# Spreading the score steps of exact attention evenly over the slots

## The chip, the cores and the metric

The kernel runs on one core of one Trainium2 chip. The metric is the device time of one execution in microseconds; lower is better. The engines are TensorE (PE in the profile, PEld its weight loads), VectorE (DVE), ScalarE (ACT), GpSimd (POOL) and SyncE (SP), whose queue issues most of the DMAs. Each engine works through its own list of instructions in order and waits on semaphores where it needs another's result.

## The reference, cut to what matters

Four layers work on x of 4 x 512 x 128 with a context of 4 x 154 x 128. The change touches the attentions of the first two layers alone: the cross attention of L0 and the causal self attention and the cross attention of L1, all with 16 heads of 8 features, softmax exact in float32.

```python
# L0: cross attention over the context
q = (target @ wq).reshape(b, tq, 16, 8); k, v likewise from the context
scores = jnp.einsum('bqhd,bkhd->bhqk', q, k) * (1.0 / np.sqrt(8))
attn = jax.nn.softmax(scores, axis=-1)
out = jnp.einsum('bhqk,bkhd->bqhd', attn, v).reshape(b, tq, d) @ wo + bo
# L1: the same twice, first causal over x itself, then over the context,
#     x = _layernorm(x + _attn(...)) after each, then a mixture of 8 experts
```

Behind them come the experts of L1, two quantised attentions and a feed-forward of L2, and a grouped attention with a feed-forward of L3. The change leaves these alone.

## The kernel before, in words

The three exact attentions times four sequences make 12 *units*, `EXACT_UNITS`: 0 to 3 are L0's cross attentions, 4 to 7 the causal self attentions, 8 to 11 L1's cross attentions. A unit has 4 *groups* of 4 heads.

Each head's scores are computed twice. A *score step* (`scores_exact`) computes scores with the queries on the partitions, only so that `top_exact` on DVE (line 1912) can take the maximum along the keys. A cross unit has 4 steps a group, each of 8 matmuls (lines 1075 and, in L0, 1079) with one reduction of 128 x 616; a self unit has 8 a group, whose widths fall with causality from 512 to 128 keys (lines 1083 and 1085), with reductions of 1024 down to 256 elements. The steps share two pairs of PSUM banks: step i waits until the reduction of step i-2 is done. When a group's last step is reduced, `split_tops` (lines 1921 to 1924, four small DVE operations) splits the maxima into bf16 parts; the item `tops` transposes them on PE (line 963) and ACT copies them out (line 1406).

The second computation has the keys on the partitions. It goes by *slots*: `scores_transposed(w)` (lines 1109 to 1113, for the context's tail 1101 and 1103) fills one of two banks with scores less the maxima, and ACT takes the exponential (line 1468). A group has 5 slots in a cross unit and 10 in a self unit, so there are 320 slots, 20 or 40 a unit. `weigh_batch` (lines 1134 and 1136) multiplies finished exponentials with the values.

PE's order in a slot is written out by hand: `scores_transposed(w)`, the score steps of the slot, the slot's items, the weighing. DVE's order is the slot's reductions (with `split_tops` behind a group's last), then the slot's items. The items of `schedule` carry the rest: K, Q and V are projections; N1, r and N2 normalise the output of the unit before (r are four reciprocals, line 1686; N2 is line 973 on PE and 1690 on DVE); W is its output projection and statistics, M and H its layer norm and transposes; R1 to R3 and G (lines 1007 and 1012) are the routing of the experts.

The steps of a group are computed during the group before: `steps_in_slot(w)` puts them into the first `PER - 3` slots of the group before. In a cross unit that is two steps in each of the group's slots 0 and 1 and none in slots 2 to 4; in a self unit one each in slots 0 to 5, two in slot 6, none in 7 to 9. `tops` stands in slot `per - 2` of the group: slot 3 of 5, or slot 8 of 10.

The first group of a unit is computed in the last group of the unit before it, so its first step needs that unit's keys and queries. These take a long way: items K and Q (slots 0 and 1 of a cross unit, 1 and 2 of a self unit), ACT copies, DVE splits each into three bf16 terms (`split`, lines 1624 to 1626), SP writes the terms to DRAM (line 791) and reads them back stacked, 16 DMAs for the keys (line 773) and then 16 for the queries (line 780). `scores_exact` with i == 0 waits for both.

In a cross unit the last group has slots 15 to 19, in a self unit slots 30 to 39. Slots are numbered from the unit's first below, unless "slot w of 320" is said.

Of the kernel before, what the change touches and what calls it, by code (L numbers as in the profile page):

```python
# [17 lines left out]
GROUPS = HEADS // 4  # L18
# [45 lines left out]
EXACT_UNITS, QUANT_UNITS = range(0, 12), range(16, 24)  # L64
# [10 lines left out]
def is_cross(u):  # L75
    return stage(u) in (L0, CROSS, QCROSS)
# [6 lines left out]
def exact_steps(u):  # L83

    if is_cross(u):
        return [(c, n) for c in range(PAIRS) for n in range(2)]

    return [(2 * g + c, n) for g in range(GROUPS) for n in reversed(range(TILES)) for c in range(2)]
# [16 lines left out]
STEP_BASE, BLOCKS, BATCHES, BATCH_BASE, FIRST_SLOT = {}, [], [], {}, {}  # L105
# [11 lines left out]
PER = {u: (5 if is_cross(u) else 10) for u in EXACT_UNITS}  # L117
PER_GROUP = {u: len(exact_steps(u)) // GROUPS for u in EXACT_UNITS}


def next_group(u, g):
    return (u, g + 1) if g + 1 < GROUPS else (u + 1, 0) if u + 1 in EXACT_UNITS else None


def steps_in_slot(w):

    u, g = BLOCKS[w][:2]
    n = (w - FIRST_SLOT[u]) % PER[u]
    to = next_group(u, g)
    if to is None:  # L130
        return []
    v, h = to
    a, b = (min(PER_GROUP[v], PER_GROUP[v] * m // (PER[u] - 3)) for m in (n, n + 1))
    return [(v, h * PER_GROUP[v] + i) for i in range(a, b)]


def weigh_in_slot(w):
# [229 lines left out]
def build(nc, io, out):  # L367
# [3 lines left out]
    with ctx:  # L371
# [384 lines left out]
        with nc.Block() as block:  # L756
# [146 lines left out]
            def _(pe):  # L903
# [242 lines left out]
                for w in range(EXACT_SLOTS):  # L1146
                    scores_transposed(w)
                    for u, i in steps_in_slot(w):
                        scores_exact(u, i)
                    for it in EXACT_ITEMS.get(w, ()):  # L1150
                        item(*it)
                    if weigh_in_slot(w) is not None:
                        weigh_batch(weigh_in_slot(w))
# [428 lines left out]
            def _(dve):  # L1582
# [348 lines left out]
                for w in range(EXACT_SLOTS):  # L1931
                    for u, i in steps_in_slot(w):
                        top_exact(u, i)
                        if (i + 1) % PER_GROUP[u] == 0:
                            split_tops(u, i // PER_GROUP[u])
                    for it in EXACT_ITEMS.get(w, ()):
                        item(*it)
# [377 lines left out]
```

How the kernel before makes its waits and increments, by code:

```python
            @once.gpsimd  # L706
# [7 lines left out]
                nc.gpsimd.memset(ctxT_tail4[:, :, :, :], 0.0)  # L714
                nc.gpsimd.memset(k_half_ctx.rearrange("p a s c k -> p (a s c k)").bitcast(fp32), 0.0)
                nc.gpsimd.memset(k_tail.rearrange("p a g k -> p (a g k)").bitcast(fp32), 0.0)
                nc.gpsimd.memset(top_cols.rearrange("p a t j c -> p (a t j c)").bitcast(fp32), 0.0)
                nc.gpsimd.memset(pad_rows, 0.0)
                nc.gpsimd.memset(zeros[:, :], 0.0)
                nc.gpsimd.memset(ones_bf[:, :], 1.0)
                nc.gpsimd.memset(picked[:, :, :].rearrange("p t e -> p (t e)"), 0.0)
                for i in range(2):
                    nc.gpsimd.memset(blocks_to[i][:, 0:EXPERTS], 0.0)
                pool.wait_ge(v_cols_cleared, 1)
                wide = v_cols.rearrange("p t (a i j) c -> p (t a) i j c", i=2, j=4)
                for i in range(2):
                    nc.gpsimd.memset(wide[:, :, i, :, 16 + HD * i:16 + HD * (i + 1)], 1.0)
# [1 line left out]
            @once.vector  # L729
            def _(dve):
                dve.wait_ge(cleared, 4)
                for j in range(4):
                    nc.vector.memset(ones[32 * j:32 * j + 3, j, :], 1.0)
                    nc.vector.memset(ones_tail[32 * j:32 * j + 3, 32 * j:32 * j + CTX_TAIL], 1.0)
# [30 lines left out]
                    def read_keys():  # L765
                        sp.wait_ge(k_out, 48 * (u + 1))
                        if u >= 2 and u != SELF * B:
                            sp.wait_ge(scoresT_ready, FIRST_SLOT[u - 1])
```

## Time and profile before

| what | us |
|---|---|
| median of three runs | 1651.88 (1650.27 to 1656.32) |
| profiled execution | 1640.09 |
| its span on the core | 1638.3 |
| mean granted TensorE clock | 0.83 |

| engine | busy us | share |
|---|---|---|
| PE | 1174.7 | 72% |
| PEld | 666.8 | 41% |
| DVE | 1100.5 | 67% |
| ACT | 901.9 | 55% |
| POOL | 678.3 | 41% |

The exact attentions take the first 614 us or so. Busy time of PE counts matmuls whose ends are modelled, so a wait between two matmuls shows only where it is longer than the pipeline. A timeline row gives start, duration, engine, line, operation, output and inputs, shapes, how many instructions it merges, and in brackets the idle time of the engine before it with what ended it. "issue" there is a wait that nothing in the profile is seen to end.

### The profile page before, as it was taken

To read this page: it belongs to the slowest core of one execution; us is meant where nothing else is said; L and a number is where in the kernel's file an instruction comes from. 1 tells how busy PE (TensorE), PEld (TensorE's weight loads), DVE (VectorE), ACT (ScalarE), POOL (GpSimd) and SP (SyncE) were. 2 spreads that over 40 slices of the span, in tenths; PEclk is the share of its full clock that TensorE was granted. 3 is DMA by queue.
4 is the path that set the end of the run, shared out by engine and by line. 5 is a ranking of instruction groups with operands and counts; after the bars stand their busy time and mean duration, and the time that the engine had idled before them with its cause. 6 is when DMAs were issued, how large, how long until landed. Compare 5 with 4: busy or idle time off the path is not lost.

```text
span 1638.3 us, 27753 instructions
## 1 busy us (share of the span) xinstructions
PE 1174.7 (72%) x8832; PEld 666.8 (41%) x8832; DVE 1100.5 (67%) x3127; ACT 901.9 (55%) x2546; POOL 678.3 (41%) x1048
## 2 busy tenths in 40 slices
PE   2698989999978788784534354544438778888888
PEld 1354445555534338782111121122215534453545
DVE  2466676676667775367989899977764566666533
ACT  1344545445544446456767778888882254545642
POOL 5201100110111141545888878877771245344420
PEclk9899999999999999896555555555559899999999
DMA  5322332120153211216655557665560112111000
GB/s 165 64 47 57 62 92 65 61 72 17 32 106 91 47 40 38 83 51 161 118 99 108 98 109 124 116 109 105 106 108 14 26 38 54 30 31 43 6 1 26
DMA packets 263825, 115.53 MB, mean 71 GB/s; under 512 B 215928, under 2 KB 252672, under 8 KB 261504
## 3 DMA queue, kind: packets, MB, share of 16 engines
q1 hardware_dynamic: 258720, 107.34, 31.3%
q0 software_dynamic: 2048, 4.20, 0.9%
q10 hardware_dynamic: 2912, 2.22, 0.4%
q8 instruction: 71, 1.16, 0.3%
q14 instruction: 74, 0.61, 0.1%
HBM read 38.54 MB, written 16.45 MB: 34 GB/s over the span
## 4 chain that ended last, share of the span: by engine, by line
PE 36%; DVE 19%; POOL 18%; issue 14%; ACT 9%; DMA 2%; SPq 1%; POOLq 0%; DVEq 0%; ACTq 0%
POOL arena L2221 10%; ACT arena L1521 5%; DVE minus_top L1912 4%; PE acc L1136 3%; PE misc L973 3%; PE trans L1109 2%; POOL inv_total L2210 2%; PE trans L1113 2%; PE misc L979 2%; PE trans L1260 2%; PE score L1272 2%; PE score L1075 2%; PE score L1274 1%; DVE top_score L1994 1%; PE score L1083 1%
## 5 line engine op out<-in xcount | busy, mean ns | idle before, releaser
L2221 POOL TENSOR_SCALAR arena<-arena,inv_total 128x512 f16<-128x512 f32 (+1 forms) x512 | 299.6, 585 | 57.4 <-DVE inv_total L1988 16.2
L1912 DVE TENSOR_REDUCE minus_top<-score 128x4 f32<-128x616 f32 (+4 forms) x256 | 197.3, 805 | 165.8 <-PE score L1079 65.2
L2084 POOL TENSOR_TENSOR rstd<-spread,minus_half 128x4 f32<-128x4 f32 x36 | 37.6, 1045 | 539.2 <-DVE spread L1602 469.9
L1521 ACT ACTIVATE arena<-score,minus_top,exp_scale 128x512 f32<-128x512 f32 (+1 forms) x340 | 210.4, 625 | 17.5 <-POOL arena L2221 7.5
L1468 ACT ACTIVATE arena<-trans 128x512 f32<-128x512 f32 x240 | 141.3, 597 | 136.0 <-PE trans L1113 133.5
L1559 ACT ACTIVATE arena<-arena,minus_top 128x154 f32<-128x154 f32 x256 | 105.1, 412 | 132.4 <-DVE minus_top L2053 132.2
L1217 PE MATMUL score<-arena 32*128 32x512 bf16 (+1 forms) x340 | 69.0, 458 | 143.2 <-ACT arena L1521 142.1
L1994 DVE TENSOR_REDUCE top_score<-score 128x2 f32<-128x1024 f32 (+1 forms) x128 | 135.6, 1060 | 0.6 <-PE score L1217 0.5
L2241 POOL TENSOR_TENSOR arena<-arena,inv_total 128x512 f32<-128x512 f32 x64 | 66.6, 1040 | 146.9 <-DVE inv_total L2061 133.0
L1113 PE MATMUL trans<-arena 128*128 128x512 bf16 (+3 forms) x384 | 123.0, 329 | 0.0
L1521 ACT ACTIVATE arena<-trans,minus_top,exp_scale 128x154 f32<-128x154 f32 (+1 forms) x172 | 105.5, 620 | 16.3 <-POOL arena L2221 11.7
L2048 DVE CUSTOM_DVE_ANT_0 arena<-score,arena 128x154 f32<-128x154 f32 x256 | 66.1, 314 | 62.8 <-PE score L1297 62.5
L1977 DVE TENSOR_SCALAR arena<-arena 128x1024 bf16<-128x1024 f16 x192 | 102.7, 535 | 6.1 <-DMA arena<-arena 6.0
L1075 PE MATMUL score<-arena 128*128 128x154 bf16 x512 | 69.3, 244 | 35.9 <-issue 27.8
L1217 PEld LDWEIGHTS score<-arena 32*128 32x128 bf16 x340 | 14.2, 102 | 194.6 <-ACT arena L1521 177.5
L1512 ACT ACTIVATE minus_top<-top_score,exp_scale 128x2 f32<-128x2 f32 (+1 forms) x192 | 56.5, 294 | 61.0 <-DVE top_score L1994 60.6
L1217 PE MATMUL trans<-arena 32*128 32x154 bf16 (+1 forms) x172 | 34.9, 454 | 71.9 <-ACT arena L1521 71.8
L1468 ACT ACTIVATE arena<-trans,arena 128x512 f32<-128x512 f32 x80 | 53.9, 689 | 56.2 <-PE trans L1113 55.4
L1136 PE MATMUL acc<-arena 128*32 128x512 f32 (+3 forms) x768 | 80.2, 505 | 2.3 <-ACT arena L1468 2.3
L1236 PE MATMUL acc<-arena 128*32 128x128 bf16 x1536 | 59.3, 307 | 28.0 <-DVE oT L2002 15.5
L1109 PE MATMUL trans<-arena,late 128*128 128x512 bf16 (+3 forms) x256 | 76.5, 301 | 0.3 <-ACT arena L1406 0.3
L1486 ACT ACTIVATE arena<-score,arena 128x128 f32<-128x128 f32 x184 | 52.2, 369 | 40.7 <-PE score L1173 40.6
(283 smaller groups left out, 3046.7 us busy)
## 6 DMA issues: line engine op xcount, KB each, us to landing
arena<-q_terms SPq DMA_DIRECT2D x176, 64.0 KB
late<-arena SPq DMA_DIRECT2D x128, 64.0 KB, 2.0
q_terms<-arena SPq DMA_DIRECT2D x36, 128.0 KB
late<-k_terms SPq DMA_DIRECT2D x64, 64.0 KB
arena<-arena SPq DMA_TRANSPOSE x192, 3.0
by_expert<-zeros SPq DMA_DIRECT2D x2, 1472.0 KB, 14.3
arena<-by_expert SPq DMA_DIRECT2D x10, 256.0 KB, 3.0
from_expert<-arena SPq DMA_DIRECT2D x10, 256.0 KB, 2.6
```

What stands on the lines that cost most here:

```text
L1075: ins = nc.tensor.matmul(dst, q_stack[:, u % 2, c, t * P:(t + 1) * P], k_half_ctx[:, u % 2, s, c, 0:CTX], start=True, stop=(stage(u) != L0))
L1109: nc.tensor.matmul(dst, keys, q_stack[:, u % 2, h // 2, q0:TOKENS], start=True, stop=False)
L1113: ins = nc.tensor.matmul(dst, ones[:, j, :], top_rows[:, g % 2, q0:TOKENS], start=False, stop=True)
L1136: ins = nc.tensor.matmul(acc[32 * j:32 * j + 32, q0:TOKENS], v_cols[:, k, 4 * g + j, :], src, start=(b % half == 0 and k == 0), stop=(last ...
L1217: ins = nc.tensor.matmul(quant_score[i % 3][:, j, z * n:(z + 1) * n], qT_codes[r:r + 32, u % 2, t * P:(t + 1) * P], k4_codes[r:r + 32, u % ...
L1468: nc.scalar.activation(expT[w % SLOTS], trans[w % 2][:, :], ACT.Exp, bias=bias)\
L1521: ins = nc.scalar.activation(probs[:, i % 3, j, of], quant_score[i % 3][:, j, of], ACT.Exp, bias=minus_top[:, at_col:at_col + 1], scale=ex ...
L1559: ins = nc.scalar.activation(gq_exp_p[:, i % 3, h, :], shifted[:, i % 3, h, :], ACT.Exp, bias=minus_top[:, at_col:at_col + 1], accum_out=t ...
L1912: nc.vector.tensor_reduce(dst, src, axis=AX.X, op=ALU.max, negate=True).then_inc(top_ready, 1)
L1977: nc.vector.tensor_scalar(pT_codes[:, of, :, :].rearrange("p k q -> p (k q)"), pT_raised[:, of, :, :].rearrange("p k q -> p (k q)"), -HALF ...
L1994: nc.vector.tensor_reduce(of_step(top_score, i), src, axis=AX.X, op=ALU.max, negate=True).then_inc(quant_top, 1)
L2221: ins = nc.gpsimd.tensor_scalar(codes[:, (i - 1) % CODE_SOURCES, j, to], probs[:, (i - 1) % 3, j, of], inv_total[:, at_col:at_col + 1], HA ...
```

## The change

A table, computed once, takes the place of the formula. The score steps of a group go one by one to evenly spaced slots of a stretch that is as long as the group in which they were, but lies `AHEAD` = 3 slots sooner.

```diff
+AHEAD = 3
+
+
+def place_steps():
+
+
+    slots = {}
+    for u in EXACT_UNITS:
+        for g in range(GROUPS):
+            to = next_group(u, g)
+            if to is None:
+                continue
+            v, h = to
+            start = FIRST_SLOT[u] + g * PER[u]
+            first, end = max(0, start - AHEAD), start + PER[u] - AHEAD
+            for i in range(PER_GROUP[v]):
+                slots.setdefault(first + ((end - first) * (i + 1) - 1) // PER_GROUP[v], []).append((v, h * PER_GROUP[v] + i))
+    return slots
+
+
+STEPS_OF_SLOT = place_steps()
+
+
 def steps_in_slot(w):
-
-    u, g = BLOCKS[w][:2]
-    n = (w - FIRST_SLOT[u]) % PER[u]
-    to = next_group(u, g)
-    if to is None:
-        return []
-    v, h = to
-    a, b = (min(PER_GROUP[v], PER_GROUP[v] * m // (PER[u] - 3)) for m in (n, n + 1))
-    return [(v, h * PER_GROUP[v] + i) for i in range(a, b)]
+    return STEPS_OF_SLOT.get(w, ())
```

Worked out: in a cross unit the four steps go from the group's slots 0, 0, 1, 1 to slots -2, -1, 0, 1 (the negative ones are slots 3 and 4 of the group before). In a self unit the eight go from 0, 1, 2, 3, 4, 5, 6, 6 to -2, -1, 0, 1, 3, 4, 5, 6. A group's last step stays in its slot, and `tops` does. At the ends of units: the first step of the next unit comes in slot 13 instead of 15 of a cross unit and in slot 28 instead of 30 of a self unit; before unit 4, whose 8 steps meet a cross unit's 5 slots, they go from 15 and 16 (four each) to 12, 13, 13, 14, 15, 15, 16, 16; before unit 8 the four go from 31, 33, 35, 36 of unit 7 to 29, 31, 34, 36. No other instruction is moved, none is added or removed.

## Rows read from the trace of the kernel before

**Rows 1.** Windows: busy us (count) of PE, PEld, DVE, ACT, POOL; clock; DMA share; GB/s.

```profile
276.00:336.00 60.00, 55.57 (x503) 31.76 (x499) 41.65 (x90) 30.79 (x53) 4.26 (x4) 1.00 0.15 49
495.40:533.10 37.70, 32.83 (x201) 15.70 (x202) 28.64 (x90) 18.24 (x36) 4.62 (x7) 1.00 0.32 71
```

**Rows 2.** PE's waits, units 1 to 11 (90.6 to 614 us): us, times, longest.

```profile
PE misc L963 <- DVE arena L1924: 15.2, 23, 1.0
PE score L1075 <- issue: 6.1, 2, 4.3
PE misc L963 <- DVE arena L1640: 5.3, 4, 2.1
PE score L1075 <- DVE minus_top L1912: 5.2, 15, 1.1
PE score L1083 <- DVE minus_top L1912: 4.9, 12, 0.8
PE misc L963 <- DVE arena L1638: 3.9, 3, 1.5
```

**Rows 3.** Timeline of PE and DVE in self unit 5, slots 16, 20 and 28.

```profile
307.34 0.23 PE L1083 MATMUL score<-late,arena 128*128 128x128 bf16 x1 [0.24 <-DVE minus_top L1912]
...
312.93 2.36 DVE L1912 TENSOR_REDUCE minus_top<-score 128x2 f32<-128x1024 f32 x2 [3.25 <-PE score L1085]
...
321.98 0.22 PE L963 MATMUL misc<-ident_bf,arena 128*128 128x128 bf16 x1 [0.58 <-DVE arena L1924]
```

**Rows 4.** Timeline of PE in cross unit 9, slots 3, 13 and 15.

```profile
503.81 0.40 PE L963 MATMUL misc<-ident_bf,arena 128*128 128x128 bf16 x4 [1.23 <-DVE arena L1640]
...
521.02 0.38 PE L1109 MATMUL trans<-arena 128*128 128x512 bf16 x1
...
522.60 0.38 PE L963 MATMUL misc<-ident_bf,arena 128*128 128x128 bf16 x4 [0.99 <-DVE arena L1924]
...
524.58 0.70 PE L1075 MATMUL score<-arena 128*128 128x154 bf16 x8
```

**Rows 5.** Timeline of DVE in cross unit 9, slot 1.

```profile
498.59 1.50 DVE L1912 TENSOR_REDUCE minus_top<-score 128x4 f32<-128x616 f32 x2
...
500.91 0.69 DVE L1624 TENSOR_TENSOR arena<-arena 128x512 f32<-128x512 f32 x1
```

**Rows 6.** SP's queue in unit 9: query terms written, then read back stacked.

```profile
502.82 1.80 SPq L791 DMA_DIRECT2D q_terms<-arena  x3
...
511.07 5.33 SPq L780 DMA_DIRECT2D arena<-q_terms  x16
```

**Rows 7.** Windows in which the query loads for units 2, 4, 10, 11 end.

```profile
119.00:120.00 1.00, 1.00 (x4) 0.30 (x4) 0.97 (x2) 0.13 (x1) 1.00 (x2) 1.00 0.28 41
199.00:200.00 1.00, 1.00 (x6) 0.40 (x3) 0.98 (x3) 0.00 (x0) 0.67 (x1) 1.00 0.42 57
522.00:523.00 1.00, 0.40 (x5) 0.35 (x6) 0.97 (x5) 0.36 (x1) 0.00 (x0) 1.00 0.28 49
562.00:563.00 1.00, 0.40 (x2) 0.00 (x0) 0.00 (x0) 0.99 (x2) 0.92 (x2) 1.00 0.08 16
```

**Rows 8.** Timeline of PE: where units 1 and 3 reach their last `tops`.

```profile
120.10 0.38 PE L1109 MATMUL trans<-arena 128*128 128x512 bf16 x1
...
200.32 0.38 PE L1109 MATMUL trans<-arena 128*128 128x512 bf16 x1
```

**Rows 9.** PE's long pauses, and the window behind the last of them.

```profile
81.32 0.29 PE L1075 MATMUL score<-arena 128*128 128x154 bf16 x1 [6.86 <-issue]
...
487.30 1.19 PE L1075 MATMUL score<-arena 128*128 128x154 bf16 x8 [4.26 <-issue]
...
564.27 0.69 PE L1075 MATMUL score<-arena 128*128 128x154 bf16 x8 [1.86 <-issue]
...
572.88 0.19 PE L1007 MATMUL misc<-picked,before_bf 128*128 128x72 bf16 x1 [2.96 <-DVE picked L1792]
...
573.90:580.70 6.80, 5.70 (x29) 2.30 (x26) 6.27 (x19) 1.79 (x3) 3.25 (x4) 0.50 0.06 19
```

## The prediction

> **What bounds the kernel now.** The change touches the first 614 of 1638.3 us; the other 1024 us keep their instructions, and I count nothing there. I read the windows by unit first. A self unit keeps PE busy for 55.57 of 60 us, cross unit 9 for 32.83 of 37.7, while DVE has 41.65 and 28.64 and ACT 30.79 and 18.24 [rows 1]. So PE sets the pace, and since no instruction is added or removed, what can be won is the time in which PE waits: some 4.4 and 4.9 us a unit. The table of PE's waits says who ends it [rows 2]. Of units 1 to 11, 15.2 us are `tops` waiting for `split_tops`; 5.3 and 3.9 are `tops` waiting for DVE to read V out of `misc`; 5.2 and 4.9 are score steps waiting for a reduction to free a bank. These 34.5 us hang on when DVE does its reductions, and they are the ceiling. Then there are 6.1 us of "issue" at L1075, in two waits. What they are comes out of the DMA windows: the queries of the next unit are not there yet. The timeline shows the same: a pause of 4.26 us ahead of unit 9's first step, 1.86 ahead of unit 11's, and 6.86 ahead of unit 1's, outside that table's stretch [rows 9].
>
> **Paired steps.** The second step of a slot pauses 0.24 us in a self unit [rows 3]. With one step a slot the reduction two steps back is at least a slot old, so I take away both bank waits, 5.2 and 4.9 us, except where three slots ahead of unit 4 keep a pair.
>
> **`tops`.** In slot 28 of a self unit it pauses 0.58 us for `split_tops` [rows 3]; cross unit 9 has 0.99 in slot 13 [rows 4]. The last step stays in its slot, but it has no twin before it: DVE has one reduction less, 0.75 us in a cross unit (1.50 for two) [rows 5]. And a step of the next group now stands between `scores_transposed` and `tops`, 0.27 us of work in a cross unit, 0.54 in a self unit's wide ones. Together they close both pauses. The work that hides it is that step; without it 0.3 us of each would stay.
>
> **V.** The wait of 1.23 us in slot 3 [rows 4] is for DVE, which does reductions, the splits of K and of Q, then V. Two reductions now lie in the unit before, one each in slots 0 and 1 remain. PE comes 1 us sooner too, so most of the wait stays; the position at `tops` moves by 1.1 us and one step more is done by then. Bounds 0 and 1.5; 1.1 is nearest to 1.50 less the part that PE itself gains.
>
> **The added wait.** Steps now stand in slots 8 and 9 (cross 3 and 4) of a group. Their reductions lie on DVE between the reciprocals r and N2's product, which item W on PE waits for, and behind W the next slots' transposed scores. In a self unit these are the widest, 1.2 us each (2.36 for two) [rows 3]. PE spends 1.1 us of its own on the same two steps ahead of N2, so between 0 and 2.4 us I take 0.65 a self unit, 0.4 a cross unit.
>
> **Self units.** Four `tops` of about 0.55 and bank waits of 0.75 in sum (0.24 and a longer one) make 2.95; less 0.65: 2.3 us. Four units: -9.2 us.
>
> **Cross units that need wait for nothing.** Of the 5.2 us of bank waits [rows 2] a unit has 0.74 before slot 13 and 0.47 behind it. By slot 13 that is 0.74 and V's 1.1, less 0.4: 1.45. Then 0.99 and 0.47 more: 2.9. Unit 2, whose queries have slack, gives -2.8. Unit 11 computes no next unit: -1.3.
>
> **The queries' load.** A moved step takes its condition along. Unit 9 ran unit 10's first step at 524.58 without a pause [rows 4]. The load's traffic ends at 522.6 (0.28 of a rate near 0.5 in that window) [rows 7]. From traffic's end to a waiting step it is 2.1 us: for unit 11 it ends at about 562.15 [rows 7] and the step runs at 564.27 [rows 9]. So unit 10's queries counted from 524.3 or so. The step moves to slot 13: 521.02 plus 0.43 for the transposed scores is 521.45 [rows 4], less 1.45 and the two steps that no longer come before it (0.54): 519.5. The load moves as well, since Q's split ran from 500.91, behind a pair of reductions at 498.59 [rows 5], and the writes at 502.82 and reads at 511.07 hang on it [rows 6]. One reduction less and PE's 0.2 make 0.95 us (bounds 0 and 1.5): 523.3. PE, which runs in order, stands still for 3.8 us, and the work of two slots that used to hide the load stands behind it: `tops`, the transposed scores of slots 14 and 15 and H, which run from 522.60 to 524.58, 1.98 us [rows 4]. So the point reached at 524.58 + 0.27 = 524.85 is reached at 523.3 + 0.27 + 1.98 = 525.55. The rest has two steps more (0.54) and the pair's 0.47 less. Unit 9: +0.8, where it would have won 2.9.
>
> By the same working: unit 1 reaches the place at 120.53 - 1.99 = 118.5 [rows 8]; its load's traffic ends at 119.6 [rows 7], so 119.6 + 2.1 - 0.95 = 120.7: a pause of 2.2; it passes that point at 122.95 instead of 120.53 + 3.4 = 123.9 and wins 0.9. Unit 3 gets there at 200.75 - 1.99 = 198.8 [rows 8], the load at 200.0 + 2.1 - 0.95 = 201.1 [rows 7]; it also loses most of the 2 us of bank waits among its eight steps: -2.4. Self units have slack: the load counts some 29 us behind a unit's start (524.3 less 495.4), and slot 28 of 40 in 60 us comes at 42 or later [rows 1]. Units 0 and 8 pause already (6.86 and 4.26) [rows 9] and pause about 2 and 3 us longer: +1.2 (unit 0's load is not sooner) and +0.8. Unit 10 had 1.86; its +0.8 ends in the pause of 2.96 that waits for the routing on DVE [rows 9], whose end stays; the paired steps behind that one gain: -1.5.
>
> **The clock.** Behind the pause of 2.96 us the granted clock is 0.50, the lower level of 1.2 GHz, for 6.8 us [rows 9]; behind 4.26 us eight score matmuls take 1.19 us, behind 1.86 only 0.69 [rows 9]. So a pause between 1.86 and 2.96 us is where it turns, and it costs up to half of 6.8, 3.4 us. I charge 1.3 more for unit 0, 1.2 for unit 8 (the work of 1.98 now runs at half) and 1.4 for unit 9 (a new 3.8). Unit 10's falls into a pause that is there anyway; units 1 and 3, at 2.2 and 2.3, I leave free.
>
> The Trainium skill bears on this (TensorE: Matmul & The Clock Gate, HAM oscillation): waits for a DMA between short stretches of matmuls make the engine start each stretch at the lower clock, and it advises to arrange the work so that the engine isn't left waiting. By that rule moving the first step ahead of its load is the wrong direction; it is the third rival.
>
> **Sum.** Units 4 to 7, 2, 11, 1, 3 and 10: -9.2 - 2.8 - 1.3 - 0.9 - 2.4 - 1.5 = -18.1; units 0, 8 and 9: 2.5 + 2.0 + 2.2 = +6.7; together -11.4 us. The span of 1638.3 becomes 1626.9, the profiled execution of 1640.09 some 1628.7. That execution lies 11.8 us below the median of the three runs, 1651.88; against the median I predict 1640.5.
>
> **Rivals.** First, the pauses go back less far: self units and units 2 and 11 gain their 13.3 us, but the loads land as late as now and units 0, 8, 9, 10, 1 and 3 end at +2.5, +2.8, +3.5, +1, +1.3 and 0: -2.2, or 1649.7. For it speaks that Q's 16 reads follow 16 reads of keys in one queue, whose pace a reduction doesn't change. Second, the loads bind less: they vary (the queries of unit 10 ended about 11.5 us behind the first read at 511.07 [rows 6, 7]) and the clock stays up, so only the added pauses remain: -20, or 1632. Third, the other side: every pause behind a moved first step takes the clock down. Units 1, 3 and 10 pay 3.4 each (10.2), unit 0 once more 3.4, units 8 and 9 the rest of theirs (3.5), and the loads are no sooner (3.8): -11.4 + 20.9 = +9.5, 1661.4. It decides from the length at which the clock falls: if 2.2 us is enough, this is what comes; against it speaks only the 1.86 that cost nothing. Fourth, the change doesn't do what it says: the last step and `tops` stay where they are, the first step comes two slots sooner, not three, and pairs remain ahead of unit 4. If `tops` waits for DVE as before, only the bank waits of 10.1 go, and the holds take 6: -4, 1648.
>
> **How the numbers follow.** The forecast has 0.5, of which 0.08 would end within 0.5% of the time before (8.3 us, about what a measurement of this kernel can tell from no change); the first rival 0.25, the second 0.12, the third 0.08, the fourth 0.05. Faster: 0.42 + 0.12 = 0.54, say 0.55; same 0.08 + 0.25 + 0.05, say 0.37; slower 0.08. The range reaches from beyond the second rival, 1627, to past the first one's price and half of the way to the third, 1655.
>
> **What would show it.** Self units of 57.7 us instead of 60; no waits of score steps for `minus_top` but ahead of unit 4; `tops` without waits for L1924; a wait of W for `oT` of 0.4 to 0.65. Ahead of the first steps of units 10 and 11 "issue" of about 4 us, in units 1 and 3 of about 2, at unit 9 above 7, and the clock at 0.50 behind each that is over 2.9. Wrong it would be if self units stay at 60 (then DVE's order costs PE what the spreading gives), or if cross units 8 to 10 grow by more than 3 us each.

## The result, and the profile after

| what | before | after |
|---|---|---|
| median, runs on one chip | 1651.08 us (20 runs, 1640.47 to 1659.52) | 1634.31 us (20 runs, 1621.35 to 1647.99) |
| ratio of the two | 1 | 0.9904, 95% interval 0.9882 to 0.9927 |
| profiled execution / its span | 1640.09 / 1638.3 | 1633.61 / 1631.8 |
| mean granted TensorE clock | 0.83 | 0.825 |

The change makes the kernel about 1.0% faster, 16.8 us by the medians. The two profiled executions differ by 6.5 us only. They can be laid side by side: cut where PE starts each unit's first transposed scores, the exact attentions take 573.7 us before and 563.2 after, 10.5 less. What stands ahead of them takes 40.9 and 41.8 us, and what follows, whose instructions are the same, 1023.7 and 1026.8. In the profiles of this study that following part lies anywhere from 1023.7 to 1035.4 us, so the before profile is at its lower end. Below I compare units, not spans.

| us of each unit | 0 | 1 | 2 | 3 | 4 | 5 | 6 | 7 | 8 | 9 | 10 | 11 |
|---|---|---|---|---|---|---|---|---|---|---|---|---|
| before | 49.7 | 40.3 | 42.4 | 41.4 | 61.3 | 60.0 | 60.0 | 57.7 | 41.7 | 37.7 | 40.7 | 40.8 |
| after | 51.8 | 40.0 | 38.3 | 39.6 | 59.0 | 57.9 | 57.9 | 55.8 | 41.6 | 40.5 | 41.5 | 39.5 |
| pause ahead of the next unit's first step, before | 6.9 | 0 | 0 | 0 | 0 | 0 | 0 | 0 | 4.3 | 0 | 1.9 | |
| the same, after | 10.1 | 2.3 | 1.1 | 2.2 | 0 | 0 | 0 | 0 | 7.5 | 6.0 | 4.2 | |

All lines of the code named in the change's surroundings are 15 higher after it (1912 is 1927, 1924 is 1939, 1075 is 1090, 1083 is 1098, 963 is 978). First the windows of the kernel after, self unit 5 and cross unit 9; they answer [rows 1], with the same columns.

```profile
275.80:333.70 57.90, 55.17 (x500) 31.88 (x498) 42.83 (x91) 30.71 (x53) 4.25 (x4) 1.00 0.17 51
483.60:524.00 40.40, 32.61 (x202) 17.21 (x200) 28.51 (x88) 18.06 (x36) 4.61 (x7) 0.92 0.27 52
```

In the self unit PE does the same 55 us of work in 2.1 us less; in the cross unit it does the same 32.6 in 2.7 us more, and the granted clock is 0.92 instead of 1.00.

PE's waits in the kernel after, units 1 to 11 (93.6 to 606 us), answer [rows 2]: us, times, longest.

```profile
PE score L1090 <- issue: 21.0, 5, 7.5
PE misc L930 <- DVE normed L1633: 3.3, 4, 0.9
PE misc L978 <- DVE arena L1939: 3.0, 3, 2.1
PE misc L978 <- DVE arena L1655: 2.8, 3, 1.5
...
PE misc L925 <- DVE arena L1764: 2.7, 4, 0.7
PE score L1090 <- DVE minus_top L1927: 2.4, 1, 2.4
PE score L1098 <- issue: 2.2, 1, 2.2
...
PE misc L1003 <- DVE oT L1705: 1.3, 3, 0.4
```

`tops` waiting for `split_tops` falls from 15.2 us to 3.0, V's waits from 5.3 and 3.9 to 2.8 and 1.0. The waits for score banks fall from 10.1 to 2.6 (2.4 and a row of 0.2). Of those 34.5 us that I had called the ceiling, some 25 are gone. In their place the wait for the query loads, "issue", has grown from 6.1 to 23.2 us.

The pauses themselves stand in PE's timeline of the kernel after: the first steps of units 1, 2, 3, 4, 9, 10 and 11. They answer [rows 9]. A score step of L1's cross units is 4 matmuls, not the 8 that the description of the kernel gives for every cross unit (that is right in L0 alone): x4 here is one step, and x8 in the rows of the kernel before is a pair.

```profile
83.57 0.29 PE L1090 MATMUL score<-arena 128*128 128x154 bf16 x1 [10.09 <-issue]
...
122.72 0.23 PE L1090 MATMUL score<-arena 128*128 128x154 bf16 x1 [2.28 <-issue]
...
162.67 0.23 PE L1090 MATMUL score<-arena 128*128 128x154 bf16 x1 [1.05 <-issue]
...
198.63 0.40 PE L1098 MATMUL score<-late,arena 128*128 128x512 bf16 x1 [2.25 <-issue]
...
473.32 0.67 PE L1090 MATMUL score<-arena 128*128 128x154 bf16 x4 [7.54 <-issue]
...
513.31 0.67 PE L1090 MATMUL score<-arena 128*128 128x154 bf16 x4 [5.96 <-issue]
...
552.21 0.67 PE L1090 MATMUL score<-arena 128*128 128x154 bf16 x4 [4.22 <-issue]
```

What each does to the clock is read from windows of the kernel after, laid on the stretches at or behind the pauses of 2.28, 1.05, 2.25 and 7.54 us (the last begins inside its pause, so only 5.38 of its 10.20 us hold work of PE); the clock is the third number from the right.

```profile
123.80:127.20 3.40, 3.40 (x17) 2.25 (x15) 1.26 (x2) 1.75 (x3) 2.87 (x8) 0.50 0.00 0
162.60:166.00 3.40, 3.33 (x37) 2.76 (x38) 2.80 (x8) 2.03 (x4) 1.92 (x2) 1.00 0.15 52
198.90:202.30 3.40, 3.40 (x15) 1.69 (x14) 2.60 (x6) 0.69 (x1) 0.27 (x1) 0.50 0.01 2
468.50:478.70 10.20, 5.38 (x27) 3.66 (x28) 1.83 (x3) 2.56 (x4) 2.33 (x5) 0.50 1.03 251
```

Behind 2.28 and 2.25 us the clock is at its lower level, 1.2 GHz; behind 1.05 it is not. In sum PE's clock is at 0.50 for 51.2 us of the exact part after the change and 27.3 before.

Last, SP's queue in unit 9 of the kernel after, and three windows at the end of that load's traffic; they answer [rows 6, 7].

```profile
489.88 1.80 SPq L806 DMA_DIRECT2D q_terms<-arena  x3
491.78 6.17 SPq L788 DMA_DIRECT2D arena<-k_terms_ctx  x16
498.05 5.37 SPq L795 DMA_DIRECT2D arena<-q_terms  x16
...
510.00:511.00 1.00, 0.00 (x0) 0.00 (x0) 0.00 (x0) 0.00 (x0) 0.94 (x1) 0.50 0.52 82
511.00:512.00 1.00, 0.00 (x0) 0.00 (x0) 0.00 (x0) 0.00 (x0) 0.85 (x3) 0.50 0.29 49
512.00:513.00 1.00, 0.00 (x0) 0.00 (x0) 0.00 (x0) 0.00 (x0) 0.54 (x2) 0.50 0.04 8
```

Counted from unit 9's start (483.6; 495.4 before), the writes go out at 6.3 us (7.4 before) and the first read at 14.5 (15.7 before), 1.1 and 1.2 sooner. But the traffic ends at about 28 (27.2 before), and the step runs at 29.7. In this unit the load was sent off sooner and did not come sooner. It is not so in each: where the step waited for it in both kernels, it runs at 31.3 us from the start of unit 8 (33.6 before) and at 28.1 from that of unit 10 (31.2 before), but at 41.8 from that of unit 0 (40.4 before).

### The profile page after: what moved, and what is told of

Read it like the earlier page. It is cut to its first block, busy times and chain, and to the rows that moved or that the text cites. A ratio compares the mean times of both kernels' runs of the same rounds, so it can differ in the third digit from the quotient of the medians.

```text
span 1631.8 us, 27753 instructions
## 1 busy us (share of the span) xinstructions
PE 1165.1 (71%) x8832; PEld 676.5 (41%) x8832; DVE 1109.7 (68%) x3127; ACT 903.4 (55%) x2546; POOL 677.9 (42%) x1048
## 3 DMA queue, kind: packets, MB, share of 16 engines
q1 hardware_dynamic: 258720, 107.34, 31.2%
q0 software_dynamic: 2048, 4.20, 0.9%
## 4 chain that ended last, share of the span: by engine, by line
PE 39%; POOL 19%; DVE 15%; issue 15%; ACT 8%; DMA 2%; SPq 1%; another core or an unknown queue 0%; POOLq 0%; ACTq 0%; DVEq 0%
POOL arena L2236 10%; ACT arena L1536 5%; PE acc L1151 3%; PE trans L1124 3%; PE trans L1128 3%; POOL inv_total L2225 2%; PE misc L988 2%; PE misc L994 2%; PE score L1098 2%; PE trans L1275 2%; PE score L1090 2%; DVE minus_top L1927 2%; POOL arena L2183 2%; PE score L1287 2%; PE score L1289 2%
## 5 line engine op out<-in xcount | busy, mean ns | idle before, releaser
L2236 POOL TENSOR_SCALAR arena<-arena,inv_total 128x512 f16<-128x512 f32 (+1 forms) x512 | 299.6, 585 | 57.3 <-DVE inv_total L2003 16.4
L1927 DVE TENSOR_REDUCE minus_top<-score 128x4 f32<-128x616 f32 (+4 forms) x256 | 204.2, 804 | 150.9 <-PE score L1094 61.2
L1536 ACT ACTIVATE arena<-score,minus_top,exp_scale 128x512 f32<-128x512 f32 (+1 forms) x340 | 210.4, 625 | 17.5 <-POOL arena L2236 7.5
L1536 ACT ACTIVATE arena<-trans,minus_top,exp_scale 128x154 f32<-128x154 f32 (+1 forms) x172 | 105.5, 620 | 16.3 <-POOL arena L2236 11.7
L1090 PE MATMUL score<-arena 128*128 128x154 bf16 x512 | 74.2, 244 | 51.9 <-issue 45.8
L1090 PEld LDWEIGHTS score<-arena 128*128 128x128 bf16 x512 | 49.0, 104 | 79.7 <-issue 52.4
L1501 ACT ACTIVATE arena<-score,arena 128x128 f32<-128x128 f32 x184 | 51.9, 371 | 49.8 <-PE score L1188 42.4
L1251 PE MATMUL acc<-arena 128*32 128x128 bf16 x1536 | 58.6, 304 | 28.1 <-DVE oT L2017 15.5
```

Source lines behind the costliest of these rows:

```text
L1090: ins = nc.tensor.matmul(dst, q_stack[:, u % 2, c, t * P:(t + 1) * P], k_half_ctx[:, u % 2, s, c, 0:CTX], start=True, stop=(stage(u) != L0))
L1536: ins = nc.scalar.activation(probs[:, i % 3, j, of], quant_score[i % 3][:, j, of], ACT.Exp, bias=minus_top[:, at_col:at_col + 1], scale=ex ...
L1927: nc.vector.tensor_reduce(dst, src, axis=AX.X, op=ALU.max, negate=True).then_inc(top_ready, 1)
L2236: ins = nc.gpsimd.tensor_scalar(codes[:, (i - 1) % CODE_SOURCES, j, to], probs[:, (i - 1) % 3, j, of], inv_total[:, at_col:at_col + 1], HA ...
```

## The experiments

Each kernel is the changed one with the edit shown, but for "The same load with the old placing", which is the kernel before with that edit. The kernel before was measured again beside each set of runs, so "against" has three values (1644.09, 1648.42 and 1656.27 us) and only ratios can be compared across sets. "Cross 1 to 3" and the like are sums over the unit times of its profile; before they are 124.1 (cross 1 to 3), 239.0 (self 4 to 7) and 160.9 (cross 8 to 11), after 117.9, 230.6 and 163.1.

**Which placing pays: inside units.** The new placing where the placed group belongs to the same unit, the formula of before for a next unit's first group, so that no first step moves.

```diff
+    for w in range(EXACT_SLOTS):
+        u, g = BLOCKS[w][:2]
+        if next_group(u, g) and not (g < GROUPS - 1):
+            slots.setdefault(w, []).extend(old_steps(w))
...
-            if to is None:
+            if to is None or not (g < GROUPS - 1):
```

> The new placing for the groups inside a unit, the old one (slots 15, 15, 16, 16 of a cross unit, 30 to 36 of a self unit) for the first group of the next unit. If the first steps' wait for their queries is what the change loses (10.1, 2.3, 1.1, 2.2, 7.5, 6.0 and 4.2 us in the changed kernel's trace), the pauses ahead of units 1, 9 and 11 go back to 6.9, 4.3 and 1.9 us, those ahead of 2, 3, 4 and 10 to none, and the time falls below the changed kernel's: -24 us against the kernel before, ratio 0.985. If the gain comes from beginning the next unit sooner, it is less than the changed kernel's: -9, ratio 0.994.

Measured: 1626.6 us against 1644.09, ratio 0.9886 (0.9843 to 0.9928). Cross 1 to 3: 115.6; self: 232.1; cross 8 to 11: 160.3; unit 0: 50.9. That is 17.5 us less than before where I expected 24. The intervals of this kernel and of the whole change overlap, so the timing alone does not say which is faster. The unit times do say where the gain is: the placing inside the units takes 14.8 us off the exact part, where the whole change takes 10.5. And the load holds PE up here too, although its first steps stand in their old slots:

```profile
PE score L1105 <- issue: 12.5, 3, 4.5
```

(PE's waits of this kernel, 93.6 to 606 us.) Three pauses of 4.5, 4.2 and 3.7 us in front of units 9, 10 and 11, where before had 4.3, none and 1.9; ahead of unit 1 it is 8.3, where before had 6.9. PE gets to slot 15 2.5 to 3.0 us sooner in each of the three; the load comes 2.7 us sooner in unit 8 and 0.7 in unit 10, and later in unit 9. The same kernel again, on another chip:

> One more look at the placing of e1_inside, for its pauses: with this placing the first steps stand in slot 15 again, but e1's trace still showed 4.5, 4.2 and 3.7 us ahead of units 9, 10 and 11. If the load ends a fixed time behind a unit's start (some 29 us in a cross unit) and PE merely gets there sooner, the pauses come again within 1.5 us of that, and the units last 38 to 41 us. If they were an accident of one load, two of the three are below 2 us.

It gave one execution of 1632.91 us, with cross 1 to 3 at 117.3, self at 232.1, cross 8 to 11 at 159.5. The pauses came again, 3.0, 4.1 and 3.4 us: they are no accident of one load. Between these two executions of one program the cross units repeat to about 2 us in a sum of 120 to 160, the self units to 0.1.

**The opposite.** The same edit with the condition turned round (`g == GROUPS - 1`): only the next unit's first group is placed anew.

> The counterpart: the old placing inside units, the new one only for the first group of the next unit. If the wait for the queries is a loss, this kernel is slower than the one before: cross units 0, 8, 9 and 10 get longer pauses and little in return, the self units win 0.6 us each from the one group; +6 us, ratio 1.004. If the sooner beginning is a gain of its own: -6, ratio 0.996.

Measured: 1653.5 against 1644.09, ratio 1.0061 (1.0029 to 1.0094): slower. Self 237.5, cross 1 to 3 122.0, cross 8 to 11 169.3, unit 0 53.9. In the self units the two halves add up: 6.9 and 1.5 us are the change's 8.4. In cross 8 to 11 moving the first steps alone costs 8.4 us against the profile before (4.3 against the next experiment's, which has the same code there); in cross 1 to 3 it wins 2.1. Its waits, same stretch:

```profile
PE score L1105 <- issue: 16.2, 4, 5.8
PE misc L993 <- DVE arena L1954: 7.3, 14, 0.8
```

So half of the change, the early first step, is a loss by itself in a cross unit whose load is late.

**Self units alone.** Condition `not is_cross(u)`: new placing in units 4 to 7 only.

> The new placing only for the groups that are computed during self units 4 to 7. By the sum of the prediction these units give 2.3 us each, -9 us, ratio 0.9945, at 57.7 us a unit instead of 60, and the cross units keep their times to 0.3 us. If the self units' gain in the changed kernel came from work that the neighbours had taken over, the ratio is nearer 1.

Measured: 1636.49 against 1644.09, ratio 0.9963 (0.9932 to 0.9994). The self units are at 230.3 us, 8.7 less than before, and cross 1 to 3 at 124.5, as before. 0.37% of 1644 is 6.1 us with an interval of 1 to 11; the 8.7 lie in it. But cross 8 to 11, whose code is that of before, takes 164.9 us and not 160.9: I expected 0.3 at most, and it is 4.0. Unit 9 alone takes 40.2 for 37.7. Its load of unit 10's queries took 15.5 us from the first read to the step, and PE paused, where in the profile before the step ran 13.5 us behind the first read without a pause:

```profile
503.05 5.35 SPq L810 DMA_DIRECT2D arena<-q_terms  x16
...
518.59 1.06 PE L1105 MATMUL score<-arena 128*128 128x154 bf16 x8 [1.78 <-issue]
```

So from one profile to another, differences of some 4 us in cross 8 to 11 and 2.5 in unit 9 need no change of their code. They can come from when a load ends and what the clock does then (20.5 us at 0.50 in these four units here, 13.7 before).

**The load out of the way.** The changed placing, with the queries read back in two parts. The first two head pairs, which are group 0's, come first with a semaphore of their own, and the first step waits for them alone; the others are waited for ahead of group 1's first step.

```diff
+                            if side == "q":
+                                sp.wait_ge(q_first, 16 * 2 * len(terms) * u)
...
-                    if u == 0:
-
-                        read_queries(slice(0, 2), q_first)
-                    read_queries(slice(0 if u else 2, PAIRS), q_stacked)
+                    read_queries(slice(0, 2), q_first)
+                    read_queries(slice(2, PAIRS), q_stacked)
...
-                        if u:
-                            pe.wait_ge(q_stacked, 32 * len(Q_TERMS) * (u + 1))
-                        else:
-                            pe.wait_ge(q_first, 32 * len(Q_TERMS))
+                        pe.wait_ge(q_first, 32 * len(Q_TERMS) * (u + 1))
...
-                    if u == 0 and i == PER_GROUP[0]:
-                        pe.wait_ge(q_stacked, 32 * len(Q_TERMS))
+                    if i == PER_GROUP[u]:
+                        pe.wait_ge(q_stacked, 32 * len(Q_TERMS) * (u + 1))
```

> The changed placing, but every unit's queries are read back in two parts, the two head pairs of group 0 first (as unit 0 does already), and the first step waits for that part alone; the second part is waited for by the first step of group 1, in slot 18 of the unit before. 16 DMAs more a unit for SP (5.3 us). If the wait for the queries is the loss, the pauses ahead of units 9, 10 and 11 shrink by 4 us or more and the time is -28 us against before, ratio 0.983. If SP's queue is what makes the load late, the pause moves to slot 18 and little is won over the changed kernel: -16, ratio 0.990.

Measured: 1603.73 against 1644.09, ratio 0.9742 (0.9698 to 0.9786), faster than both kernels: 2.6% below before, where I expected 1.7. Units: 0 at 46.1; cross 1 to 3 at 111.3; self 230.6, to the tenth as in the changed kernel; cross 8 to 11 at 141.3. PE's waits for the queries in it, 93.6 to 600 us:

```profile
PE score L1087 <- DMA arena<-q_terms: 2.5, 2, 2.2
PE score L1087 <- issue: 1.6, 1, 1.6
```

The 23.2 us are down to 4.1 (the 2.2 of them is a wait for the second part), and the pause ahead of unit 1 from 10.1 to 2.9. Each part is again 16 DMAs; the first part's are a quarter as large. The same row of both pages, DMA issues, the changed kernel's first and then this one's for the first part:

```profile
arena<-q_terms SPq DMA_DIRECT2D x176, 64.0 KB
```

```profile
arena<-q_terms SPq DMA_DIRECT2D x192, 16.0 KB
```

From the first read's issue to the step it is now 7.0 to 7.1 us where the step waits (in units 0 and 9, for units 1 and 10), of which the issue of 16 DMAs is some 5.5. In the changed kernel it is 14.1 to 15.3, and 17.5 in unit 8, in whose window above the DMA engines are full, 1.03 and 251 GB/s; weights of an expert, one transfer of 2048 KB and four of 256, are issued right behind that unit's reads.

**The same load with the old placing.** Is the 2.6% the load's alone?

> The old placing of the steps, with the queries read back in two parts as in e4_q_first. It tells how much of e4's 40 us is the load alone. If the load only costs the pauses that the kernel before shows (6.9, 4.3 and 1.9 us ahead of units 1, 9 and 11) with their half clocks, this is -16 us, ratio 0.990, self units stay at 60 us and cross units 8 and 10 fall to 37 or so. If SP's longer queue pays for part of it: -8. If the two-part load alone were the whole of e4: -40, ratio 0.975, and the placing worth nothing beside it.

Measured: 1636.57 against 1648.42, ratio 0.9913 (0.9882 to 0.9944). Cross 1 to 3: 124.2, self 239.1, cross 8 to 11: 156.8, no pause ahead of any first step. Its waits, 93.6 to 606 us:

```profile
PE misc L963 <- DVE arena L1921: 15.4, 23, 1.2
PE score L1072 <- DVE minus_top L1909: 7.5, 19, 2.3
PE score L1080 <- DVE minus_top L1909: 4.9, 12, 0.8
```

The rows of [rows 2] are back. The two changes together do more than their sum:

| us | unit 0 | cross 1 to 3 | self 4 to 7 | cross 8 to 11 |
|---|---|---|---|---|
| placing alone | +2.1 | -6.2 | -8.4 | +2.2 |
| load alone | -6.4 | +0.1 | +0.1 | -4.1 |
| both | -3.6 | -12.8 | -8.4 | -19.6 |

In units 8 to 11 the placing alone gives nothing (+2.2 against the profile before, -1.9 against the 164.9 of the same code in "Self units alone") and the load 4.1, both give 19.6; this sum stands clear of the 4 us by which the profiles differ, the two parts alone don't. There the placing's gain is swallowed by the pause in which PE waits for the next unit's queries: what PE saves ahead of it, the pause gives back, and the clock takes more.

**Is the early first step worth anything once the load is away?** Two-part load, placing of the first experiment (new inside units, old slots for the next unit's first group).

> The two-part load of e4_q_first with the placing of e1_inside: the first group of the next unit in its old slots, in pairs. With the load out of the way the sooner and even beginning of that group is tested by itself. If it gains as inside a unit (bank waits, tops), this kernel is slower than e4 by 0.4 us a self unit and 1 to 1.5 us a cross unit: -33 against before, ratio 0.980. If the sooner beginning gives nothing even then: as e4, -40, 0.9745.

Measured: 1614.18 against 1648.42, ratio 0.9776 (0.9743 to 0.9809). Its units sum to 542.5 us, those of the full placing to 529.2. The two ratios (0.9776 and 0.9742) have overlapping intervals, so the 13 us of the profiles are not confirmed by the timing; both point the same way. In the self units, where no load meets a first step, the sooner group is worth 1.5 us (232.1 and 230.6), the same as without the two-part load.

**The load later.** The item Q of the changed kernel one slot later.

```diff
-                at(exact, f + (1 if u else 3), ("Q", nxt))
+                at(exact, f + (2 if u else 4), ("Q", nxt))
```

> The changed kernel with item Q one slot later in cross units (slot 2 instead of 1, slot 4 instead of 3 in unit 0), so that the load starts some 3.5 us later: a dose of the suspected cost. If the load sets the cross units' time, the pauses ahead of units 1, 2, 3, 4, 9, 10 and 11 grow by about 3 us each, and the time by 20: ratio against before 1.002. If the pauses in the changed kernel are covered by other waits, under 8 us are added: 0.995 or less.

Measured: 1666.29 against 1648.42, ratio 1.0098 (1.0064 to 1.0133). PE's waits, 93.6 to 606 us:

```profile
PE score L1090 <- issue: 39.8, 5, 12.0
PE score L1098 <- issue: 5.3, 1, 5.3
```

The cross units, unit 0 among them, are 37.9 us longer than in the changed kernel (exact part 601.1 for 563.2). Seven of them load queries for the next unit; unit 11, which loads none, has 3.8 of the 37.9 us, so it is 4.9 us a load. Moving Q by one slot sent the first read off 3.1 to 4.0 us later, counted from the unit's start (1.0 in unit 0). The pauses alone grow by 23.6 us, 3.4 each (all of them, 57.0 for 33.4), about as forecast; part of the rest is the clock, at 0.50 for 81.9 us instead of 51.2. The time grows more than the 20 us that I expected: by the two ratios it is 32. The self units are again at 230.6.

**Spread or sooner.** The two-part load, `AHEAD` 1 and 2 instead of 3: the steps are as evenly spread, but a group's last step stands in the slot of its `tops`, or one ahead of it, not two.

> Two-part load of the queries kept (as in e4_q_first), and the score steps still spread at most one a slot, but each group's last step stands in the slot of its own tops (AHEAD = 1 in place of 3), so the first step too is two slots later than in e4. It separates 'spread' from 'sooner'. Theory A (what pays is that the last step, its reduction and its split are over before the tops are due): every one of the 47 tops waits again for a reduction and a split, some 1.4 to 1.7 us more each; the waits for score banks stay gone. About 1604 + 47 x 1.4 = 1670 us, ratio about 1.01 to 1.02 to the kernel before. Theory B (what pays is the spacing of the steps, which frees the banks): within 0.5% of e4, ratio 0.974 to 0.98.

> As e4_q_first, with the last step one slot ahead of the tops (AHEAD = 2). Theory A: a slot of a self unit is some 3.7 us and of a cross unit some 2.4 us, against a reduction and split of about 2.5 to 3 us behind a step, so the self units keep nearly all and the cross units lose up to 0.5 us at a tops: 32 x 0.3 = 10 us, ratio about 0.98. Theory B: no change to e4, 0.974. Rival: the load no longer meets the first step at all, so the holds of e4 (2.9 and 1.6 us) vanish, worth 0.3% less, 0.972.

Measured: `AHEAD` 1: 1745.91 against 1656.27, ratio 1.0553 (1.0519 to 1.0587). `AHEAD` 2: 1658.83, ratio 1.0016 (0.9989 to 1.0044). Both are slower than forecast by either theory. The waits of `tops` for `split_tops` over the whole exact part (47 groups), first in the kernel with 1, then with 2:

```profile
PE misc L978 <- DVE arena L1936: 121.8, 47, 5.1
```

```profile
PE misc L978 <- DVE arena L1936: 52.1, 40, 1.8
```

With 3 it is 2.9 us in 7 waits. Spreading is worth nothing if the last step is not two slots ahead of `tops`. For `AHEAD` 2 my estimate went by slots of 3.7 and 2.4 us; that was an error, since a self unit of 60 us has 40 slots, 1.5 us each, and a cross unit of 38 has 20, 1.9 each. With those lengths the 1.3 us a wait (52.1 / 40) is a little under what one slot less takes away, as it should be. The exact part grows by 51.7 us over `AHEAD` 3 (580.9 and 529.2), about the rows' 49 and V's 9 less the 9 or so that the waits for the queries no longer take. For `AHEAD` 1 I had 1.4 to 1.7 us a wait; it is 2.6, and the rows explain 119 us of the 146 by which the exact part grows. The clock bears on what is left: behind these waits it falls again and again, 26 stretches and 116.0 us at 0.50 in the exact part, against 17.1 us with `AHEAD` 3. One of the waits and the window behind it, in the kernel with 1:

```profile
464.00 0.38 PE L978 MATMUL misc<-ident_bf,arena 128*128 128x128 bf16 x4 [2.56 <-DVE arena L1936]
...
464.60:468.00 3.40, 3.40 (x8) 1.30 (x5) 0.07 (x1) 1.00 (x2) 0.00 (x0) 0.50 0.22 48
```

**Sooner still.** `AHEAD` 4, with the two-part load.

> As e4_q_first, with every step one slot sooner still (AHEAD = 4). Theory A: nothing is left to gain at the tops, and the first step of a unit meets the end of even the shortened load: pauses of 1 to 3 us ahead of the first step in the cross units where e4 had none, 0 to 15 us in all, ratio 0.974 to 0.983. Theory B: also no gain, and no loss if the load is early enough, 0.974.

Measured: 1612.9 against 1656.27, ratio 0.9735 (0.9704 to 0.9766); with 3 it was 0.9742. No difference can be told. Self 227.9, 2.7 less than with 3; cross 8 to 11: 150.7, against 141.3; exact part 538.6 and 529.2. The self units gain 2.7 us and the cross units lose 12 in the profile, which the timing doesn't show; V's wait is a small part of it:

```profile
PE misc L978 <- DVE arena L1652: 5.9, 4, 2.2
```

(3.5 us with 3.)

## Why the prediction was right, and where it was wrong

The time came out 16.8 us below before by the medians, where I had 11.4, and 1634.3 where I had 1640.5; the profiles' exact parts give 10.5. Against the profiles the sum is good to a microsecond. Much of that is luck: the terms of units 8 and 10 missed by 2.1 and 2.3 us in opposite directions, and the same code in units 8 to 11 differs by 4 us between two profiles, so agreement there to a microsecond proves little.

**Right: the self units.** 2.3, 2.1, 2.1 and 1.9 us against 2.3 each, and most of it seen in the rows of units 4 to 7: no wait for a score bank left (3.0 us before), `tops` waits down from 9.1 to 0.9 us, all of PE's waits there from 17.7 to 11.7. The experiment with self units alone has them at 230.3, and no edit of the load changes them by more than 0.1. The added wait was in the wrong place: I had 0.65 us a self unit for W behind `oT`, and no such wait shows there (in the cross units it does, 0.4 at most, as forecast). PE waits instead at line 925 for DVE, 2.7 us in four waits, which before had no row, and at line 930, 3.3 us where it was 2.0: 1.0 more a unit. In unit 5 neither is my mechanism, a reduction ahead on DVE. What PE waits for there is itself at the end of a chain over POOL, for which DVE stands idle:

```profile
295.54 1.12 DVE L1633 TENSOR_SCALAR normed<-y,moments,rstd 128x128 f32<-128x128 f32 x4 [0.26 <-POOL rstd L2099]
...
300.66 0.29 DVE L1763 TENSOR_SCALAR arena<-arena,ctx_rstd 128x128 f32<-128x128 f32 x1 [0.56 <-POOL ctx_rstd L2188]
```

PE comes sooner and the chain doesn't.

**Right: the pauses, nearly all.** I had 2.2, 2.3, about 9, over 7 and about 4 for units 1, 3, 0, 8 and 10; measured are 2.3, 2.2, 10.1, 7.5 and 4.2. Not foreseen was the 1.05 ahead of unit 3: I had given unit 2's queries slack. Units 0 (+2.1 for +2.5) and 9 (+2.8 for +2.2) and 11 (-1.3 for -1.3) came out as worked, unit 9 by luck: with the placing of before it takes 40.2 us in "Self units alone", and 40.5 here. That a sooner first step runs into its load was the right term, and the runs bear it out from both sides: Q one slot later costs 37.9 us, the load out of the way gives 34.0 us (563.2 less 529.2).

**Wrong: the load comes 0.95 us sooner.** The step said that one reduction less on DVE brings the load forward. It brought its issue forward, by 1.1 to 1.2 us in unit 9, but not its end: 13.6 us from the first read to the end of traffic instead of 11.5. So the pause was 6.0 us for my 3.8. This was the condition of my first rival, and in unit 9 it holds; in units 8 and 10 the load came 2.3 and 3.1 us sooner, more than my 0.95. What was wrong is to take one load's length for all: the 11.5 was that of one of the quickest. From first read to a step that waits, unit 9's load takes 15.3 us here, 16.2, 16.0 and 16.4 in the kernels with one half of the change (one of them run twice), and 15.5 with the placing of before in "Self units alone"; over all units and kernels with the whole load it is 13.5 to 19.0. In units 1 and 3 the pauses are those that I had worked out with the 0.95.

**Wrong: units 8 and 10.** For unit 8 I charged +2.0, for a pause about 3 us longer and a clock that falls; both came (3.3 us longer, 10.2 us at 0.50), and yet the unit takes 41.6 us, -0.1. I had gains of 2.9 in it as elsewhere, so it has won some 2 us more than that; before, its own pause of 4.26 us already had 6.8 us at half clock behind it. Of those 2 us, 1.3 are the load, 2.3 us sooner for my 0.95. I have no row that names the rest. For unit 10 I had -1.5 and it is +0.8: the step at fault is that its longer pause "ends in the pause of 2.96 that waits for the routing". The pause grew by 2.4 us and took the clock down for 6.8 us, while the one for the routing shrank only to 2.12, and the bank wait behind it that I had wanted gone is 2.37 us, where it was 1.09 before:

```profile
564.42 0.19 PE L1022 MATMUL misc<-picked,before_bf 128*128 128x72 bf16 x1 [2.12 <-DVE picked L1807]
...
569.24 0.44 PE L1090 MATMUL score<-arena 128*128 128x154 bf16 x4 [2.37 <-DVE minus_top L1927]
```

It waits for a reduction that DVE starts at 568.38, behind the routing's operations, and not for a twin step. The old placing has it too, 2.31 us in "Self units alone" and 2.32 with the two-part load; with the two-part load and the new placing it is 0.70. So it depends on when the step comes, and the placing alone doesn't remove it.

**Wrong: the clock's turning point.** I took it for one length between 1.86 and 2.96 us and let the pauses of units 1 and 3, of 2.2 to 2.3, go free. Both took the clock down, for 3.4 us each. And there is no one length: in the same kernel a pause of 2.37 us, the last row above, left the clock up. Here is the window behind it:

```profile
569.30:572.70 3.40, 3.40 (x22) 1.59 (x23) 2.17 (x7) 0.94 (x2) 2.48 (x4) 1.00 0.17 58
```

So the third rival's condition came true in part; what was wrong in it is the price. It charged 3.4 us for each pause, half of a stretch of 6.8. Behind the pauses of units 1 and 3 the stretch is itself 3.4 us, and since PE works on at half the clock, at most 1.7 of it is lost; unit 10's is 6.8, at most 3.4. Of units 1 to 3 I had -6.1 and they gave -6.2: unit 1 less (-0.3 for -0.9), unit 3 less (-1.8 for -2.4), unit 2 more (-4.1 for -2.8). The Trainium skill (TensorE: Matmul & The Clock Gate, HAM oscillation) describes such a pattern, short stretches of matmuls between waits for a DMA, which start at the lower clock time after time. This case's trace agrees that it happens: 27.3 us at 0.50 have become 51.2. It doesn't bear out that the change must lose by it.

**The fourth rival did not come true.** `tops` does not wait as before; the two slots from last step to `tops` are enough, and the runs with one slot and none show that these two, which the change leaves as they were, carry everything.

**Open.** The medians differ by 16.8 us, the exact parts of the profiled executions by 10.5. The interval of the ratio reaches from 12.1 to 19.5 us. The 19 and 27 us by which single executions of the two kernels differ lie partly in the part that no edit touches (1023.7 to 1035.4 us in the profiles), so one pair of profiles can't settle the 6 us between. What makes one load of the queries 2 us longer than another, in unit 9 or elsewhere, no run shows. How much of the cross units' time is the pause itself and how much the clock behind it isn't separated by any run either.

## What to carry to other kernels

Work placed sooner takes its condition along. When the bank and reduction waits of a PE-bound loop have gone, look at once for what sets the period of the whole loop, here the 14 to 17.5 us from the first read of the next unit's operands to their use; split that load so that the first user waits for its own part alone, and the placing's gain, that was nothing clear in units 8 to 11, becomes 15.5 us. Where a producer's last step is followed by a chain on another engine, count the slots between the two in microseconds: two slots left 2.9 us of waits in the whole exact part, one left 52, none 122. And profile the untouched program twice before reading a microsecond out of a unit: here four unchanged units differed by 4.

## What the runs showed of the hardware

- At every pause of PE of 3 us or more between the end of unit 0 and that of unit 11, in all of these profiles, the granted clock went to 0.50: for 3.4 to 10.2 us at pauses of 3.0 to 7.2 us, and for 10.2 or 13.7 us at 7.5 to 12.0. Between 1.5 and 2.9 us its length alone doesn't tell. The wait for the bank behind the routing is 2.37 us in the changed kernel, in that of new placing inside units and in the one with Q later; the first keeps its clock, the two others lose it for 3.4 us. V's wait in unit 8 is 2.10 us in the kernel before, where nothing falls, and 2.10 in that with the two-part load alone, where it falls. In the two executions of the program with new placing inside units, a wait of 1.47 us in unit 8 kept the clock once and lost it for 3.4 us the other time, and the exact parts have 31 and 41 us at 0.50. The exact parts take 558.9 and 561.5 us, so the clock may be a part of why executions of one program differ; what decides isn't shown by any run.
- With `AHEAD` 2 there were 40 waits of up to 1.8 us for `split_tops` and only two stretches at 0.50 in the whole exact part, one of them behind a wait of 3.36 us. Waits of 1.3 us in the mean cost their length and hardly any clock.
- Sixteen reads of 64 KB, issued in 5.4 us on one queue, take 14.1 to 15.3 us in the changed kernel from the first issue to the step that needs them all (17.5 beside the weights of an expert, 13.5 to 19.0 over all kernels); sixteen of 16 KB, issued in as long, 7.0 to 7.2. So behind the last issue it is about 9 us in the one case and 1.5 in the other: most of what the step waited for goes with the size of the reads, not with their number. Whether bytes or packets set it isn't told apart.
